# A decoder of twelve stages on one core: expert results sent home block by block with an indirect DMA, loaded back plainly, under a new order of steps

## The reference

```python
top_k_probs, top_k_idx = jax.lax.top_k(router_probs, TOP_K)      # TOP_K = 2, E = 8
...
for e in range(E):
    h = new_gelu(x_flat @ w1[e].T + b1[e])                       # 128 -> 512
    out_e = h @ w2[e].T + b2[e]                                  # 512 -> 128
    output = output + cw[:, e:e + 1] * out_e
```

## Time and profile before

| | |
|---|---|
| median of three runs | 2,279.9 us |
| the profiled execution | 2,300.3 us, span 2,298.5 us, mean granted clock 0.89 |
| PE busy | 1,805.3 us (79%) |
| DVE busy | 1,420.6 us (62%) |
| ACT busy | 1,051.3 us (46%) |
| POOL busy | 358.8 us (16%), 324 instructions |
| DMA | 228.48 MB, mean 99 GB/s |

### The profile page before, as it was taken

How to read it: one execution, slowest core, us unless ns; L and a number is a source line. 1 busy time by engine, 2 the same in 40 slices (tenths; PEclk the granted TensorE clock), 3 DMA queues, 4 the chain that set the end, 5 groups by cost and what they waited for, 6 DMA issues and landing times.

```text
span 2298.5 us, 40299 instructions
## 1 busy us (share of the span) xinstructions
PE 1805.3 (79%) x14664; PEld 1401.9 (61%) x14664; DVE 1420.6 (62%) x4850; ACT 1051.3 (46%) x2820; POOL 358.8 (16%) x324
## 2 busy tenths in 40 slices
PE   6587899999994876769998888989859557765682
PEld 5455686767762644547896677666549435644682
DVE  5578525787774866767767656766652356568422
ACT  2266525676663765664122445544325236521340
POOL 3300100000002000000103000001530464123114
PEclk9899999999996987879999899999769769975796
DMA  4224190000006786683002323331027424232263
GB/s 163 72 73 117 63 361 1 1 1 1 1 1 177 202 241 184 175 240 115 1 1 52 90 63 98 77 82 40 20 71 216 130 76 103 76 110 78 96 211 93
DMA packets 213421, 228.48 MB, mean 99 GB/s; under 512 B 16212, under 2 KB 187116, under 8 KB 212584
## 3 DMA queue, kind: packets, MB, share of 16 engines
q1 hardware_dynamic: 209128, 217.51, 32.5%
q0 software_dynamic: 4096, 8.40, 1.3%
HBM read 130.86 MB, written 94.58 MB: 98 GB/s over the span
## 4 chain that ended last, share of the span: by engine, by line
PE 43%; DVE 24%; DMA 15%; POOL 5%; ACT 4%; issue 4%; SPq 4%; another core or an unknown queue 1%; DVEq 0%; POOLq 0%; ACTq 0%
PE banks L677 38%; DMA stacks<-region 6%; SPq L2549 4%; DMA skew<-region 3%; DVE P L1742 3%; DVE region L1806 2%; ACT P L1421 2%; PE banks L992 2%; DVE region L1742 2%; POOL route L2518 1%; DVE P L1996 1%; POOL sorted_x L2431 1%; DVE negm L1753 1%; DMA P<-skew 1%
## 5 line engine op out<-in xcount | busy, mean ns | idle before, releaser
L1421 ACT ACTIVATE P<-P,negm 128x256 f32<-128x256 f32 x512 | 253.8, 498 | 112.0 <-DVE negm L1976 55.7
L2391 POOL TENSOR_TENSOR rstd<-rstd,pows 128x2 f32<-128x2 f32 x96 | 68.3, 712 | 1364.3 <-DVE rstd L1746 1363.9
L1421 ACT ACTIVATE P<-banks 128x512 f32<-128x512 f32 (+2 forms) x392 | 187.0, 510 | 181.1 <-PE banks L677 174.3
L677 PE MATMUL banks<-xnT,region 128*128 128x256 f32 x672 | 182.7, 388 | 6.4 <-ACT xnT L1421 5.0
L1753 DVE TENSOR_REDUCE negm<-banks 128x2 f32<-128x512 f32 (+1 forms) x264 | 149.9, 590 | 44.6 <-PE banks L677 41.7
L677 PE MATMUL banks<-kz,qs 128*128 128x256 bf16 (+1 forms) x512 | 131.0, 289 | 48.8 <-DMA kz<-stacks 25.3
L677 PE MATMUL banks<-bands,identb 128*128 128x160 bf16 (+1 forms) x768 | 148.6, 255 | 0.0
L677 PE MATMUL banks<-region 128*32 128x256 f32 (+6 forms) x922 | 127.0, 360 | 20.8 <-ACT region L1421 9.6
L677 PE MATMUL banks<-qv,region 128*128 128x256 bf16 (+2 forms) x512 | 116.4, 270 | 29.4 <-ACT P L1421 14.4
L677 PEld LDWEIGHTS banks<-xnT,region 128*128 128x128 f32 x672 | 122.7, 193 | 26.2 <-ACT xnT L1421 9.9
L677 PE MATMUL banks<-qs,kz 128*128 128x256 bf16 (+2 forms) x512 | 117.8, 271 | 24.9 <-ACT P L1421 18.4
(11 more groups left out here) (289 smaller groups left out, 4505.8 us busy)
## 6 DMA issues: line engine op xcount, KB each, us to landing
stacks<-region SPq DMA_DIRECT2D x178, 192.0 KB, 3.0
skew<-region SPq DMA_DIRECT2D x64, 256.0 KB
sorted_x<-qs SPq DMA_DIRECT2D x2, 5120.0 KB
sorted_y<-qs SPq DMA_DIRECT2D x2, 5120.0 KB
qs<-stacks SPq DMA_DIRECT2D x24, 408.0 KB
kz<-stacks SPq DMA_DIRECT2D x48, 192.0 KB
skew<-region SPq DMA_DIRECT2D x64, 128.0 KB
skew_room<-skew SPq DMA_DIRECT2D x32, 256.0 KB, 3.8
```

The costliest lines, as they stand in the source:

```text
L677: return p.e.matmul(o, lhsT, rhs, start=start, stop=stop)
L1421: return a.e.activation(o, i, f, **kw)
L2391: g.e.tensor_tensor(room[:, :, 0], room[:, :, 0], pows[:, :], ALU.pow).then_inc(done, 1)
```

## The change

It has two parts.

1. **The way back.** The two tensors sorted_x and sorted_y of each stream become two tensors sorted_x, one per expert stage, with rows of 130 values in place of 128. The two new values are the row's home: where in a new tensor `back` its first pick's result belongs, and its first pick's row number. When DVE has turned a block's rows, it computes for each row its home (one comparison and one addition, `block_to`). After the block's result is evicted, POOL sends it home with one indirect DMA. The results then lie in the order of the tokens, and SP loads an item's 256 KB with one plain DMA. SP no longer stores results. Rows that hold no token carry their own number, so that they land in the first 128 rows of `back`.
2. **The order.** TURNS is new on all five engines.

Beside these: `further_blocks` sums the biases in two instructions, constants are one column read as a broadcast, and the clearing of the sorted tensors writes runs of 520 values.

```diff
+SORTED_W = D + 2
+BACK = 128
 TURNS = {
-    "tensor": ("11113200110023001100310047002100110012002100130015003100210032002100240014001100110062002100240012001001500200"
+    "tensor": ("11113200120022001100310047002200220021001800120062004100280012008200210026001002100150010042040100100301011020"
...
-        self.sorted_x, self.sorted_y = (nc.dram_tensor(f"sorted_{k}{n}", (SORTED_ROWS, D), F32).ap() for k in "xy")
+        self.sorted_x = [nc.dram_tensor(f"sorted_{k}{n}", (SORTED_ROWS, SORTED_W), F32).ap() for k in range(2)]
+        self.back = nc.dram_tensor(f"back{n}", (BACK + 2 * ROOM, D), F32).ap()
...
-                for e in range(E):
-                    own = mine_of[:, :, e:e + 1].to_broadcast([128, MORE, FT])
-                    b_e = b1[:, e * FT:(e + 1) * FT].unsqueeze(1).to_broadcast([128, MORE, FT])
-                    part = (tmp[:, 32:32 + MORE * FT] if e else s.block_b[:, :, :].rearrange("p q f -> p (q f)")).rearrange("p (q f) -> p q f", f=FT)
-                    i = tt(part, own, b_e, ALU.mult)
...
+                each = tmp[:, 512:512 + MORE * FT * E].rearrange("p (q f e) -> p q f e", f=FT, e=E)
+                b_e = b1.rearrange("p (e f) -> p f e", f=FT).unsqueeze(1).to_broadcast([128, MORE, FT, E])
+                step(tt(each, mine_of.unsqueeze(2).to_broadcast([128, MORE, FT, E]), b_e, ALU.mult))
+                red(s.block_b[:, :, :], each, ALU.add).then_inc(s.placed, 1)
...
                 v.e.tensor_copy(s.block_xT[:, n % 6, :], s.T[:, 0:128]).then_inc(s.turned, 1)
+                if n == E:
+                    v.wait_ge(s.placed, (ITEMS + 2) * (w + 1))
+                at = SORT["first_rows"][:, n:n + 1] if n < E else s.block_at[:, n - E:n - E + 1]
+                stt(s.block_to[:, n % 6:n % 6 + 1], s.block_rows[:, n % 8, D + 1:], at, s.block_rows[:, n % 8, D:D + 1], ALU.is_equal, ALU.add)
...
-                v.wait_ge(s.moved[k % 2], MOVED * w + MOVED // 2 + 64 * (k // 2 + 1))
+                v.wait_ge(s.lanes[k], lane_base(w + 1, k))
...
         def sorted_experts(w):
             def run(s, b, j):
-                m = j % ITEMS
-                yield
-                if m == 0:
-                    for k in range(2):
-                        g.wait_ge(s.stored[k], 16 * stores_before(w + 1, k))
...
-                for k in range(2):
-                    for t in range(TOK):
-                        g.e.indirect_dma_start(s.got[:, m, k, t, :], None, s.sorted_y[:, :], place(s, m, k, t)).then_inc(s.moved[m % 2], 16)
+                for n in range(BLOCKS if j % ITEMS == 0 else 0):
+                    yield
+                    g.wait_ge(s.y_out, BLOCKS * w + n + 1)
+                    to = bass.IndirectOffsetOnAxis(s.block_to[:, n % 6:n % 6 + 1], 0)
+                    g.e.indirect_dma_start(s.back[:, :], to, s.block_y[:, n % 2, :], None).then_inc(s.stored[n % 2], 16)
+                yield
...
-                    for copy in (z.sorted_x, z.sorted_y):
-                        dma(copy.rearrange("(p k r) d -> p k (r d)", p=128, r=n_rows),
-                            zeros[:, 0:n_rows * D].unsqueeze(1).to_broadcast([128, SORTED_ROWS // 128 // n_rows, n_rows * D]), skew_zero)
+                    for copy in z.sorted_x:
+                        for rows in (slice(0, 128), slice(128, SORTED_ROWS // 64)):
+                            n = rows.stop - rows.start
+                            dma(copy.rearrange("(p k r) d -> p k r d", k=16, r=4)[rows],
+                                z.empty_rows[128 - n:].unsqueeze(1).to_broadcast([n, 16, 4, SORTED_W]), skew_zero)
...
-            for n in range(BLOCKS):
+            for n in itertools.chain(range(4), range(8, MORE + 4)):
                 yield
                 d.wait_ge(s.y_out, BLOCKS * w + n + 1)
-                to = s.sorted_y[n * ROOM:n * ROOM + 128, :] if n < E else s.sorted_y[bass.DynSlice(row_of[n - E], 128), :]
-                dma(to, s.block_y[:, n % 2, :], s.stored[n % 2])
...
+            for m in range(ITEMS):
+                yield
+                for k in range(2):
+                    d.wait_ge(s.stored[k], 16 * stores_before(w + 1, k))
+                rows_of = s.back[BACK + 2 * S * m:BACK + 2 * S * (m + 1), :].rearrange("(t p k) d -> p t k d", t=TOK, k=2)
+                dma(s.got[:, m, :, :, :], rows_of, s.lanes[m])
```

More of the change, by code:

```diff
@@ L256, in layout @@
         ("upper", upper), ("room", on_all(np.tile(ROOM * np.arange(E), TOK))), ("steps", on_all(np.tile(128 * np.arange(1, E), E))),
-        ("below", on_all(np.tril(np.ones((E + 1, E)), -1))), ("block", on_all(np.arange(MORE))), ("first_row", on_all(128 * (1 + np.arange(MORE))))]
+        ("below", on_all(np.tril(np.ones((E + 1, E)), -1))), ("block", on_all(np.arange(MORE))), ("first_row", on_all(128 * (1 + np.arange(MORE)))),
+        ("back", (BACK + np.arange(128)[:, None] * 2 + np.arange(B // 2 * TOK) * 256).astype(np.float32)),
+        ("first_rows", (np.arange(128)[:, None] + ROOM * np.arange(E)).astype(np.float32))]
     packs["signs"] = [("k0", tiles(v["L0_ffn_k0"])), ("k1", tiles(v["L0_ffn_k1"])),
@@ L337, in __init__ @@
         self.S0, self.S1, self.T, self.V = self.bank
-        self.stats = sb("stats", [TOK, 6])
-        self.mv = sb("mv", [TOK, 2])
-        self.rstd = sb("rstd", [TOK, 1])
-        self.rms = sb("rms", [TOK, 1])
+        norms = sb("norms", [TOK, 19])
+        self.stats, self.O_stats = norms[:, :, 0:6], norms[:, :, 6:12]
+        self.mv, self.O_mv = norms[:, :, 12:14], norms[:, :, 14:16]
+        self.rstd, self.rms, self.O_rstd = (norms[:, :, k:k + 1] for k in range(16, 19))
         self.xn = [sb("xn", [TOK, D]), None]
@@ L485, in program @@
     identb = sbuf("identb", [128, 128], BF16)
-    pows = sbuf("pows", [128, TOK])
+    consts = sbuf("consts", [128, 3 * TOK + 2])
+    pows, twos, padmax = (consts[:, k * TOK:(k + 1) * TOK] for k in range(3))
+    half_pow, euler = (consts[:, 3 * TOK + k:3 * TOK + k + 1] for k in range(2))
     streams = [Stream(nc, n) for n in range(2)]
@@ L1760, in wide, with norm @@
             return a.unsqueeze(2).to_broadcast([128, TOK, E])
-        def norm(s, b, j, rms=False, rows=None, free=None):
+        def norm(s, b, j, rms=False, rows=None, free=None, back=None):
             xn = s.xn[j % 2] if rows is None else rows
@@ L1788, in norm @@
                 step(tt(s.rstd[:, :, :], s.rstd[:, :, :], s.rms[:, :, :], ALU.mult))
+            if back is not None:
+                v.wait_ge(load_sem["L1f"], 32)
+                v.e.tensor_copy(*back)
             for t in range(TOK):
@@ L2115, in run @@
                 top, exps = s.logits_top, s.exp_logits
-                yield from norm(s, b, j, rows=s.own_x[:, item, :, :], free=max(j - 3, 31) if w == 0 else j - 3)
+                yield from norm(s, b, j, rows=s.own_x[:, item, :, :], free=max(j - 3, 31) if w == 0 else j - 3,
+                                back=(s.own_rows[:, item, :, D], SORT["back"][:, TOK * item:TOK * (item + 1)]))
                 yield
```

237 lines of the change are left out of this document (117 added, 120 removed).

## The result

Four runs of the changed kernel took 2,215.16 to 2,223.63 us, median 2,219.79; the kernel before, on the same chip, 2,281.1. The ratio is 0.9733, with a 95% interval of 0.9698 to 0.9768: faster by 61 us, where 61 were forecast. In a later comparison, on a chip where the kernel before took 2,306.4 us, the same two kernels stood at 0.9671 (0.9653 to 0.9688).

The account below looks back on a forecast made before the run. No engine bounds all stages; L2_ffn and L3_ffn lose time to gather bursts, idle routing and a tail. 14 + 27 + 20 + 2 = 63 less, minus 3 for more indirect DMAs: 2,219 us from 2,279.9; 80% range 2,184 to 2,262.

Parts of the forecast that it names:

- The tail: End of L3_ffn: one indirect DMA and four plain loads replace 16 gathers; 14 us less, bounds 8 and 17.
- The order of L3_ffn: Stream 0's first blocks move inside stream 1's routing: 44 us less, minus 17 for interference, so 27 less.
- The interference: Interleaved blocks of stream 0 delay stream 1's routing chain, 1.2 us each: 17 us in L3_ffn, 14 in L2_ffn.
- L2_ffn: Same reordering there: 45 us less, minus 14 for interference, two thirds kept through L3_attn; 20 less, bounds 5 and 31.
- Further_blocks: Its 15 DVE sums become two; one saving counted in L3_ffn's chain, 2 us less, bounds 0 and 6.
- The burst starves the others: In L2_ffn and L3_ffn, bursts of gathers on POOL were taken to slow the other engines, mechanism unknown.
- the first rival: Overlap is given back as stream 1's routing slows; tail and 16 us of burst stalls remain gains: 2,248 us, 24 in 100.
- The rival by indirect DMAs as such: Stalls come from any indirect DMAs, so 92 spread them over the stage; 2,262 us, 8 in 100.
- the one by SP's queue: In L3_ffn stream 1's loads stand behind stream 0's four outputs in SP's queue; 2,255 us, 4 in 100.
- the slower one: Two result buffers, each free only when its indirect DMA has landed, hold the blocks; 2,296 us, 7 in 100.
- rel: Load behind the clearing, forecast at no cost under 12.8 us of cover; rival that it comes late: 2,244 us, 4 in 100.
- the rule on GpSimd's rings: DVE in two-port mode locks GpSimd out of writing DMA descriptors; 13 us of L3_ffn's gain lost, 2,232 us, 3 in 100.

Follow-up runs that it names:

- a_l3: The changed kernel with stream 0's blocks of L3_ffn behind stream 1's routing again; 2,251.45 us, 0.9859 of the kernel before.
- b_same: The kernel before, unchanged, run once more for a second profiled execution; 2,288.64 us.
- a_l2: The changed kernel with stream 0's blocks of L2_ffn behind stream 1's routing again; 2,243.76 us, 0.9827 of the kernel before.
- a_l23: The changed kernel with stream 0's blocks behind stream 1's routing in both L2_ffn and L3_ffn; 2,274.19 us, 0.9867 of the kernel before.
- a_same: The changed kernel, unchanged, timed again in a later comparison on another chip; 2,228.57 us, 0.9671 of the kernel before.
- b_plain: The kernel before with each of the 64 gathers replaced by a plain DMA of 128 consecutive rows; 2,257.16 us, 0.9894 of the kernel before.
- a_double: The changed kernel with a second indirect DMA per block, to a tensor nobody reads (184 in place of 92); 2,255.38 us, 0.9892 of the kernel before.
- a_relfirst: The changed kernel with SP loading rel before it clears the sorted tensors; 2,207.97 us, 0.9679 of the kernel before.

## Why the prediction was right, step by step

**The tail** (14 us less): 14.2 less, and its parts as in the sum within 0.4 us: 3.0 in place of 2.6 for the indirect DMA, 4.8 in place of 5 for the fourth load and the end of the sums.

**The order of L3_ffn** (27 less, bounds 33 and 9). 79 us were forecast from stream 1's last scatter to the last eviction, 80.1 measured; but of 35 blocks, not 32, at 2.3 us. The interference, 17 us, was mis-sized: 5.2 (116.9 against 111.7), below the lower bound of 10. PE had room there: it is busy 83.9 us of the routing at a granted clock of 0.74, 59.9 us at 0.64 in a_l3. The order is worth 34.3 us here, just over the upper bound, because the blocks that moved were slow ones: a_l3 has five gaps of 3.2 to 5.6 us (5.6, 3.4, 3.9, 3.2, 4.9) where stream 0, nearly alone, waits for its first loaded weights and rows. In the new order they lie under the routing. From b_same to the changed kernel routing and blocks together fall by 25.0 us, for the 27 forecast: the order brings 34.3, and a longer routing (below) and the way back take 9.3. The lower bound of 9 us doesn't follow from the terms that the prediction shows.

**L2_ffn** (20 less, bounds 5 and 31): 21.4 by a_l2, 19.4 by a_l23 against a_same. The steps to it were off, and their errors cancel: that is luck. The interference is 1.3 us (112.3 against 111.0 for the routing of L2_ffn), not 14. The stretch from the last scatter to the last eviction takes 107.3 us, not 92: 40 results stand in it, not 34, since only 6 of the forecast 12 moved, and stream 1's last twelve take 42.5 us, pause included, where 37.7 were forecast. And the stages behind it kept all of the lead (a_l2), not two thirds. POOL's clearing and power stand where the forecast put them:

```profile
1787.59 1.14 POOL L2460 DMA_INDIRECT back<-mask,block_to  x1 [3.34 <-DVE mask L2237]
1788.73 3.53 POOL L2478 MEMSET kz<- 128x4096 bf16 x1
1792.21 6.78 POOL L2533 TENSOR_TENSOR route<-route,consts 128x40 f32<-128x40 f32 x1
1799.18 1.03 POOL L2460 DMA_INDIRECT back<-mask,block_to  x1 [0.19 <-issue]
```

The evictions around it are 9.4 us apart, their neighbours 4.1 and 4.3: 5.2 us, for 5.3 forecast. But the path was another one. The late eviction stands in DVE's row behind the next stage's rotary front, which waits for the power; no result buffer is waited for:

```profile
1793.81 0.29 DVE L2237 COPY mask<-banks 128x128 f32<-128x128 f32 x1 [0.70 <-PE banks L688]
...
1799.03 0.18 DVE L1757 TENSOR_SCALAR route<-route 128x40 f32<-128x40 f32 x1 [2.88 <-POOL route L2533]
...
1803.20 0.28 DVE L2237 COPY mask<-banks 128x128 f32<-128x128 f32 x1
```

Nor is it a new wait: the kernel before has a gap of 8.2 us at the same place (1,823.4 to 1,831.6), behind its own power of 6.8 us, b_same one of 7.8, and a_l2 one of 9.6. The size was luck.

**Further_blocks and the 3 us for more indirect DMAs** were not tried alone. POOL has room with one DMA per block, and nothing shows the 3 us.

**What the total hides.** The routing of L3_ffn is 7.2 us longer in the new kernel even with stream 0's blocks behind it (111.7 in a_l3 against 104.5 in b_same), and that of L2_ffn 9.8 us (111.0 in a_l2 against 101.2). No term of mine held that, and its cause is open. Together with an order worth more than forecast it made the total right. Part of its closeness is luck: the later comparison gives 2,281.1 x 0.9671 = 2,206.

**The reading of the stalls was wrong**, though no term of the sum stood on it alone. "The burst starves the others" came from an execution with two long waits that no other has. What was slow there in every execution is a stream that runs alone, and DVE's sums in its way. With that the first rival also falls: the overlap was not given back, and the 16 us it granted to the bursts were not theirs.

**The rival by indirect DMAs as such** falls with b_plain, and with a_double, where nothing waits for something unnamed; **the one by SP's queue** falls with the tail of 13.1 us, and **the slower one** with the 3.9 us of waits. **rel** came 8.3 us later (349.6 against 341.3): the clearing went at 313 to 324 GB/s, not 405, a fifth or more off the rate. It has runs of 2,080 bytes now, but each tensor is also cleared in two pieces, of 128 and 32 rows of its outer dimension, and no run tells the two apart; a_relfirst, with the same clearing, shows 349 GB/s in this window. The window below is the changed kernel's, with the earlier trace rows for before:

```profile
285.00:325.00 40.00, 39.01 (x218) 35.11 (x217) 7.60 (x32) 9.57 (x12) 2.79 (x4) 1.00 1.03 313
```

PE waited 5.7 us for rel; the sum had nothing for it. The prediction gave the new order 3 of the 12.8 us of cover. It took 10: PE was ready for rel at 343.9 us (349.6 - 5.7), not at 354.1. As for the rule on GpSimd's rings (the Trainium skill, DMA: Bandwidth & Descriptors, SWDGE vs HWDGE vs iDMA), the 92 indirect DMAs took 957 ns at the median and 1,181 at most, so nothing held POOL up by a copy's length each time. But that is no test of the rule, and neither was the spread of the gathers: it speaks of DVE in its two-port mode, and no row shows DVE's copies of results, which read banks, in that mode.

**What the prediction did not see at all** is that its two parts need each other. It added the order's terms as if they held for any way back. Measured, the order alone gives 13 us, where under the new way back it gives 46.

## What to carry to other kernels

A wait that gathers a whole stream's results ties the order down: let two streams finish together, and their collecting lines up on one engine. Sending each block's result home as it comes takes that wait away, and only then does a better overlap pay; so price such changes together, not as a sum. And read a stall in two executions before building on it, above all one that the profile can't name.
